# Where the turns of the probabilities stand in a gated attention block: two behind each whole V tile, or one behind each half

## The reference, cut to what matters

```python
def _L0_xattn_ref(x, mask, k_cache, v_cache, wq, wk, wv, wo):
    q = jnp.einsum('bsd,ed->bse', x, wq)
    k_new = jnp.einsum('bsd,ed->bse', x, wk)
    v_new = jnp.einsum('bsd,ed->bse', x, wv)
    k = jnp.concatenate([k_cache, k_new], axis=1)
    v = jnp.concatenate([v_cache, v_new], axis=1)
    scores = jnp.einsum('bqd,bkd->bqk', q, k) * scale
    attn = jax.nn.softmax(scores, axis=-1)
    out = jnp.einsum('bqk,bkd->bqd', attn, v)
    return jnp.einsum('bqd,ed->bqe', out, wo)

x = x + jnp.tanh(g_xattn[0]) * _L0_xattn_ref(_layernorm(x), mask, ctx, ctx, wq, wk, wv, wo)
# the second part, with up_w = sign(up_weight), down_w = sign(down_weight)
hidden = relu(jnp.einsum('bsd,hd->bsh', _layernorm(x), up_w) * up_scale)
x = x + jnp.tanh(g_ffn[0]) * jnp.einsum('bsh,dh->bsd', hidden, down_w) * down_scale * output_scale
```

## Time and profile before

| | |
|---|---|
| median of 3 runs | 597.24 us (597.18 to 597.77) |
| the profiled execution | 597.95 us |
| its span, first to last instruction | 596.2 us |
| TensorE busy (matmul) | 587.2 us, 98% |
| VectorE busy | 376.9 us, 63% |
| ScalarE busy | 289.9 us, 49% |
| granted TensorE clock, mean | 0.999 |
| turns of probabilities | 128 transposes of 272 ns, 19.1 us |
| matmuls of the V tiles | 192, 51.9 us |

### The profile page before, as it was taken

One profiled execution on the slowest core, in us unless ns is written; L12 is line 12 of the kernel. 1 busy time (PEld: TensorE's weight loads), 2 busy tenths in 40 slices (PEclk: granted clock), 3 DMA queues, 4 the chain that ended last, 5 costly groups with the idle time before them and its releaser, 6 DMA issues.

```text
span 596.2 us, 7100 instructions
## 1 busy us (share of the span) xinstructions
PE 587.2 (98%) x2738; PEld 486.5 (82%) x2738; DVE 376.9 (63%) x532; ACT 289.9 (49%) x426; POOL 118.0 (20%) x111
## 2 busy tenths in 40 slices
PE   7999999999999999999999999999999999999997
PEld 6888888888888888888888888888887878888885
DVE  4699554587454587443677786755459734766654
ACT  3784521474321565221656565655659445645531
POOL 4106303003003012003011015242322003242002
PEclk9999999999999999999999999999999999999999
DMA  8713032032020143020212223020211301240011
GB/s 284 228 71 119 24 107 70 11 89 77 1 72 0 37 175 107 1 71 2 70 54 79 81 71 106 35 72 35 66 43 35 139 5 71 77 137 36 0 71 70
DMA packets 20097, 43.21 MB, mean 72 GB/s; under 512 B 4832, under 2 KB 4832, under 8 KB 19680
## 3 DMA queue, kind: packets, MB, share of 16 engines
q1 hardware_dynamic: 20064, 42.76, 21.7%
HBM read 36.45 MB, written 6.30 MB: 72 GB/s over the span
## 4 chain that ended last, share of the span: by engine, by line
PE 96%; DVE 2%; DMA 1%; ACT 1%; SPq 0%; issue 0%; ACTq 0%
PE proj L540 35%; PE score L670 19%; PE turn L655 12%; PE score L573 9%; PE score L540 7%; PE proj L655 5%; PE proj L573 4%; PE turn L532 2%; PE score L804 2%; DMA rows<-in_x 1%; PE proj L638 1%; PE turn L638 1%; DVE four_x L1189 0%; DVE rows L1652 0%; ACT hid L1099 0%; DVE scaled L1649 0%
## 5 line engine op out<-in xcount | busy, mean ns | idle before, releaser
L670 PE MATMUL score<-down_signs,hid_split 128*128 128x512 f32 x512 | 133.8, 390 | 0.3 <-ACT normed L1114 0.2
L670 PEld LDWEIGHTS score<-down_signs,hid_split 128*128 128x128 f32 x512 | 95.8, 188 | 21.4 <-ACT normed L1114 0.6
L540 PE MATMUL proj<-probsT,four_x 128*128 128x512 f32 x384 | 89.3, 391 | 0.0
L540 PEld LDWEIGHTS proj<-probsT,four_x 128*128 128x128 f32 x384 | 71.5, 188 | 14.6
L540 PE MATMUL proj<-four_x,weights 128*128 128x512 f32 x336 | 76.8, 389 | 0.0
L540 PEld LDWEIGHTS proj<-four_x,weights 128*128 128x128 f32 x336 | 63.0, 188 | 13.0
L465 POOL TENSOR_TENSOR four_x<-raw_ctx,four_x 128x2048 fp32r<-128x2048 f32 x7 | 32.6, 4657 | 189.5 <-ACT four_x L885 189.5
L1528 DVE TENSOR_TENSOR hid_split<-hid,hid_split 128x512 fp32r<-128x512 f32 x64 | 44.1, 691 | 16.2 <-ACT hid_split L1108 16.0
L540 PE MATMUL proj<-weights,four_x 128*128 128x512 f32 x192 | 51.9, 405 | 0.0
L655 PE MATMUL turn<-ops_b,up_ops 128*128 128x512 f32 x192 | 51.8, 391 | 0.0
L893 ACT ACTIVATE four_x<-proj 128x512 fp32r<-128x512 f32 x32 | 19.1, 597 | 65.8 <-PE proj L540 65.8
(11 more groups left out here) (128 smaller groups left out, 866.0 us busy)
## 6 DMA issues: line engine op xcount, KB each, us to landing
raw_w<-in_ffn_w SPq DMA_DIRECT2D x24, 512.0 KB, 3.3
raw_ctx<-in_ctx_turned SPq DMA_DIRECT2D x4, 1024.0 KB, 5.3
raw_ctx<-in_ctx SPq DMA_DIRECT2D x4, 1024.0 KB, 5.7
result<-rows SPq DMA_DIRECT2D x16, 256.0 KB, 2.0
rows<-in_x SPq DMA_DIRECT2D x3, 1024.0 KB, 7.3
turned_x<-in_x_turned SPq DMA_DIRECT2D x3, 1024.0 KB, 5.4
rows_away<-rows SPq DMA_DIRECT2D x1, 2048.0 KB, 13.3
rows<-rows_away SPq DMA_DIRECT2D x1, 2048.0 KB, 8.0
```

Of the source, the lines that this page charges most:

```text
L540: last = pe.matmul(bank, lhs(l), rhs(r), start=start and i == 0, stop=stop and i == 2)
L670: last = pe.matmul(wide(r), hid_split[:, n % HR, s, r * P:(r + 1) * P], down_signs[:, chunk_of(q), :], start=(q == 0 and s == HI), stop=(q ...
```

## The change

The turn of the first half of a row tile's pair moves from the middle of V tile r (behind its second term) to its end, ahead of the other turn. The semaphore `proj_done` of the V tile is raised at its last matmul as before. No other engine's program is touched.

```diff
                     for i, (lhs, rhs) in enumerate(v_terms(r)):
                         last = product(proj_bank(proj0(b) + r), lhs, rhs, i == 0, i == DC - 1)
-                        if i == 1:
-                            turn_probs(b, 2 * r)
                     last.then_inc(proj_done, 1)
+                    turn_probs(b, 2 * r)
                     turn_probs(b, 2 * r + 1)
```

## The result

| | before | changed |
|---|---|---|
| median | 597.18 us (21 runs) | 598.30 us (21 runs) |
| lowest and highest | 596.45 and 599.37 | 597.56 and 598.82 |
| the profiled execution | 597.95, span 596.2 | 597.98, span 596.2 |

The ratio of the changed kernel to the one before is 1.0017, 95% interval 1.0011 to 1.0023: some 1.0 us slower (0.7 to 1.4); between the medians it is 1.12 us. The forecast was 598.5, 1.24 us more.

The account below looks back on a forecast made before the run. TensorE, with 96% of the chain, was taken to bound the kernel. Terms -0.44 + 1.12 + 0.05 + 0.51 = +1.24 us on the profiled 597.95 gave 599.19, or 598.5 for the median; range 597.2 to 599.5.

Parts of the forecast that it names:

- TensorE bounds: TensorE has 96% of the chain that ended last; a wait on another engine costs nothing unless TensorE stands still.
- The win of the regrouping: From a batch's first V tile to its first attention product: less alternation saves 0.11 us, over four batches -0.44 us.
- a cost of 0.03 us for each entry into matmuls behind transposes: On TensorE, one entry from transposes into matmuls is saved for each V tile, some 0.03 us.
- T3 held behind T1's eviction: Each batch: fourth turn of probabilities waits for VectorE's late eviction of the second, same bank; 0.28 us, four times +1.12 us.
- VectorE named in the profile as releaser: In each batch, between third and fourth turn, a step of some 0.7 us instead of 0.43, released by VectorE's eviction of `turn`.
- T7 in the last batch: Last batch, eighth turn of probabilities: blocks of signs on ScalarE delay evictions, so it loads late; +0.05 us (0 to 0.15).
- The turned norms: Last batch: transposes of the next block's norms, behind the first 12 attention matmuls, start late; +0.51 us, once.
- T3 not held: Fourth turn of each batch does not wait; only the shorter alternation is left, 596.8 us, or 597.3; chance 0.21.
- A second hold in each batch: Fourth attention term or old half also waits for VectorE in each batch; 599.5 us at 0.25, 600.8 at 0.60; chance 0.17.
- The clock: Attention batches: at half the clock one V tile in each batch takes 2.84 us more, giving 609.9 us; chance 0.02.

Follow-up runs that it names:

- e2: Changed kernel with, on ScalarE in all batches, the exponential of tile 0 moved ahead of the eviction of turn 0; 597.02 us, ratio 0.9999.
- e3: e2 with two of VectorE's four norms in the last batch also moved earlier, one ahead of turn 5's low part, one behind it; ratio 0.9994.
- e9: e3 with, in the last batch, ScalarE taking a block of signs ahead of turn 2's eviction instead of behind it; 596.51 us against 596.95, ratio 0.9989.
- e10: Kernel before, each turn cut in two: two transposes behind each term of the V tile instead of four behind every second one; ratio 1.0020.
- e5: Kernel before, two turns together only behind V tile 0; one profile run, first V matmul to first attention product 14.74 us, last batch 14.75.
- e6: Kernel before, two turns together only behind V tile 1; one profile run, first V matmul to first attention product 14.46 to 14.49 us, last batch 14.63.
- e8: Changed kernel with the exponential of tile 1 too ahead of ScalarE's evictions of V tile 0 and turn 1; 602.90 us against 597.02, ratio 1.0089.
- e1: The changed kernel measured again, unaltered, against the kernel before; 598.36 us against 596.98, ratio 1.0020.
- e7: Kernel before, two turns together only behind V tile 3; one profile run, 598.64 us against 597.02.

## Why the prediction was right

- *TensorE bounds, and only its own time and holds count.* Right: the 1.18 us lie in TensorE's stretches from V0 to A and in the turned norms of the last batch, as summed below.
- *The win of the regrouping, -0.44.* Measured where nothing is held, in batches 0 to 2 of e2 and e3: 14.39 instead of 14.51, so -0.12 a batch, -0.48. In e9 it is 14.39 to 14.42; from V0 to the next V0 it is 87.93 to 87.96 there, 87.96 in e2 and e3, and 88.07 before, which is 0.11 to 0.15 a batch. The size was right, its reason was not, and that is luck: I wrote of a cost of 0.03 us for each entry into matmuls behind transposes, and in e10 eight more entries cost 0.04 together. What the trace shows is in the last section.
- *T3 held behind T1's eviction, 0.28 a batch.* 14.68 - 14.39 = 0.29, four times: +1.16 (forecast +1.12; my own times gave 149.21 - 148.92 = 0.29, where I wrote 0.28). Shown by e2 (order undone, hold gone), e5 and e6 (T0's place alone makes it) and e8 (it grows one for one). The 0.12 us from VectorE's end to the weight load was met exactly. What I gave as a sign, VectorE named in the profile as releaser, was not there; only the step between starts showed the hold.
- *T7 in the last batch, +0.05.* 14.78 - 14.68 = 0.10, and 0.14 in e1. The place was right. Missing in the sum was the transfer of the signs: it lands 11.96 us behind V0, in e1 12.00, and the signs start 0.02 later. Without it they would have started 0.49 behind V2's eviction (329.04), at 329.53 and not at 329.60.
- *The turned norms, +0.51.* 0.42 in the changed kernel, and 0.52 in e7, where it stands alone. The difference is A: T7's hold had put it 0.10 later already. The norms hang on T6 and not on A, 4.10 us behind T6 in both runs. I had added two holds that partly overlap.
- *Sum.* -0.48 + 1.16 + 0.10 + 0.42 = +1.20, measured 1.18 in the profiles, 1.12 between the medians and 1.0 (0.7 to 1.4) by the ratio, forecast 1.24.
- *The rivals.* T3 not held: refuted. A second hold in each batch, at the fourth attention term: not there, though my sum left it 0.02 us of slack. V0 to A can't show it, since that term stands behind A; but in batch 1 the low part of V3 ends at A + 1.76, and the term's weight load starts at A + 1.93, in step with its neighbours. And from V0 to the next V0 the three batches take 0.15 to 0.18 us more than before, and V0 to A alone takes 0.17 to 0.18 more. The clock: 1.00 in every stretch up to TensorE's last matmul, before and after; the mean of 0.999 comes from the last two microseconds, when TensorE is done.

What I missed is that ScalarE and VectorE had room to give all of it back: I read each fixed order as given, and did not ask which instruction on it stands idle ahead of the one that is late.

## What to carry to other kernels

When turns or products on a full TensorE are regrouped, what matters is when each one's result reaches the engines behind it. An instruction that is moved later drags along everything that stands behind its eviction in another engine's fixed order: here a 1.1 us exponential. Before such a move, look on these engines for idle time ahead of the eviction, and put the work queued behind it there: three moves turned +1.2 us into -0.5.

## What the runs showed of the hardware

After a turn, TensorE's matmuls of 512 columns run a little slower for a while, and then at full pace, at a granted clock of 1.00, the level of 2.4 GHz. The first twelve attention matmuls of the last batch, before the change, in two halves:

```profile
332.80 1.64 PE L540 MATMUL proj<-probsT,four_x 128*128 128x512 f32 x6
```

```profile
334.27 1.53 PE L540 MATMUL proj<-probsT,four_x 128*128 128x512 f32 x6
335.64 0.38 PE L638 MATMUL turn<-ident,normed 128*128 128x128 f32 x2
```

The first six behind the turn take 1.47 us, the second six 1.37, like the six of V0 with no turn ahead (1.36). Most of the 0.10 is no loss. The turn's last transpose, and the matmuls from the second on:

```profile
332.77 0.27 PE L532 MATMUL turn<-ident,probs 128*128 128x128 f32 x1
```

```profile
333.12 1.32 PE L540 MATMUL proj<-probsT,four_x 128*128 128x512 f32 x5
```

The first matmul starts 0.03 behind the last transpose, where transposes are 0.11 apart, and the second starts 0.32 behind the first, where matmuls are 0.227 apart. One gives back what the other takes, 0.08 to 0.09, so the change of kind by itself costs next to nothing. What is left are the steps of the matmuls behind: up to the seventh 0.229 to 0.236, then 0.227. That is 0.02 to 0.03 us for a block of six. So with turns behind every third or every sixth matmul nearly all are slow ones (e10 and before: 1.82 and 1.83 for six and four); with twelve in a row some are not (3.61 to 3.65 for twelve and eight, where twice 1.83 is 3.66). That fits e10, where a fixed cost for each entry does not. What slows them the runs do not tell, nor why the pace recovers sooner behind some pairs (3.61) than behind others (3.65).

A hold of TensorE shows in the profile as less idle time than it is, since the instruction ahead of it is drawn past the start that the next one would have had. The holds read from the starts are 0.35 us (T7 in e10's last batch), 0.37 (the turned norms of the changed kernel) and 1.39 (T3 in e8, 1.83 less 0.44); the idle time shown is 0.19, 0.22 and 1.23, each 0.15 or 0.16 less. The 0.24 to 0.26 of T3 in the changed kernel shows as none at all, only as a merged row that is too long and a weight load put down to "issue".
